# An RWKV-6 layer with a ternary-weight feed-forward: each weight load cut into two or four DMAs

## The reference

```
h = layernorm(x)
xr, xk, xv, xw = tm_* h + (1 - tm_*) h_prev          # token shift
r = sigmoid(xr Wr^T); k = xk Wk^T; v = xv Wv^T; w = -softplus(-(xw Ww^T)) - 1e-4
per head of 64:  o_t = r_t (s + exp(u + k_t) v_t^T);  s = exp(w_t) s + k_t v_t^T
x = x + (groupnorm(o) * ln_w + ln_b) * r  Wo^T
h = layernorm(x)
x = x + bitlinear(silu(bitlinear(h, w_gate)) * bitlinear(h, w_up), w_down)
```

## Time and profile before

| | us |
|---|---|
| median of 2 runs | 13519.63 |
| lowest, highest run | 13518.7, 13520.57 |
| profiled execution | 13554.92 |
| its span, slowest core (core 2) | 13553.3 |
| spans of the 8 cores | 13446.1 to 13553.3 |

### The profile page before, as it was taken

How to read it: one execution, slowest core, us unless ns; L and a number is a source line. 1 busy time by engine, 2 the same in 40 slices (tenths; PEclk the granted TensorE clock), 3 DMA queues, 4 the chain that set the end, 5 groups by cost and what they waited for, 6 DMA issues and landing times.

```text
span 13553.3 us, 44159 instructions; the slowest of 8 cores (13446.1 to 13553.3 us)
## 1 busy us (share of the span) xinstructions
PE 2850.1 (21%) x14044; PEld 1163.0 (9%) x14220; DVE 4326.3 (32%) x3858; ACT 2275.1 (17%) x2088; POOL 170.7 (1%) x60
## 2 busy tenths in 40 slices
PE   0000000012223231323132313241324031412231
PEld 0000000001101110111011101110111010101010
DVE  0010101013263416241624172407240724163326
ACT  0011011113111211121112112210221022102210
POOL 0000000000000000000000000000000000000000
PEclk9999999995666566657565756575657565756576
DMA  2221212220111011101110111010101010101011
GB/s 51 56 70 50 79 51 87 61 71 10 39 33 59 10 40 33 58 10 45 29 56 10 47 29 56 9 53 24 56 9 55 21 56 16 56 25 44 16 56 31
DMA packets 880152, 563.77 MB, mean 42 GB/s; under 512 B 610096, under 2 KB 807088, under 8 KB 877872
## 3 DMA queue, kind: packets, MB, share of 16 engines
q1 hardware_dynamic: 874160, 550.44, 14.0%
q0 software_dynamic: 5760, 10.49, 0.5%
HBM read 424.21 MB, written 52.43 MB: 35 GB/s over the span
## 4 chain that ended last, share of the span: by engine, by line
DVE 28%; SPq 19%; PE 18%; ACT 14%; DMA 14%; issue 4%; DVEq 2%; POOL 1%; ACTq 0%; POOLq 0%; another core or an unknown queue 0%
DVE arn L1394 6%; SPq L363 6%; PE ps L1292 5%; DMA arnb<-wqtu 4%; PE ps L1299 4%; DVE arn L1392 3%; SPq L225 3%; ACT L1312 2%; SPq L473 2%; SPq L1247 2%; PE ps L1447 2%; SPq L1414 2%; SPq L806 2%; DMA arnb<-arnb 2%; PE ps L568 2%
## 5 line engine op out<-in xcount | busy, mean ns | idle before, releaser
L1292 PE MATMUL ps<-arnb 128*128 128x512 bf16 x2000 | 680.6, 497 | 2557.5 <-DMA arnb<-wqtu 1960.9
L1447 PE MATMUL ps<-arnb 128*128 128x512 bf16 x2008 | 534.5, 430 | 2624.9 <-DMA arnb<-arnb 1712.1
L1322 DVE SCALAR_TENSOR_TENSOR arn<-ps,arn 128x512 f32<-128x512 f32 x256 | 192.2, 751 | 2673.8 <-ACT arn L1312 2673.8
L1394 DVE TENSOR_TENSOR arn<-arn 128x2048 f32<-128x2048 f32 x384 | 880.1, 2292 | 29.6 <-issue 1.3
L1312 ACT ACT_TABLE_LOAD x256 | 328.4, 1283 | 2489.5 <-PE ps L1299 2489.5
L568 PE MATMUL ps<-arnb 128*128 128x512 bf16 x1505 | 408.1, 422 | 1299.8 <-DMA arnb<-wtr 1207.4
L349 DVE SCALAR_TENSOR_TENSOR arnb<-arn,thr,arnb 128x1024 bf16<-128x1024 f32 (+1 forms) x72 | 118.1, 1640 | 1666.4 <-ACT arnb L337 1666.4
L1299 PE MATMUL ps<-arnb 128*128 128x512 bf16 x2016 | 544.6, 416 | 3.0 <-issue 1.5
L333 ACT ACT_TABLE_LOAD x72 | 92.4, 1283 | 2582.4 <-DVEq L310 1084.2
L280 PE MATMUL ps<-cpool_s,arn 128*1 128x1 f32 x6 | 0.6, 163 | 2373.8 <-DVE arn L274 2373.8
L1392 DVE TENSOR_SCALAR arn<-arn 128x2048 f32<-128x2048 f32 x384 | 471.2, 1227 | 30.0 <-issue 0.9
(11 more groups left out here) (163 smaller groups left out, 6037.1 us busy)
## 6 DMA issues: line engine op xcount, KB each, us to landing
arnb<-wqtg SPq DMA_DIRECT2D x64, 1024.0 KB, 5.5
arnb<-wqtu SPq DMA_DIRECT2D x64, 1024.0 KB, 8.0
arnb<-wqtd SPq DMA_DIRECT2D x64, 1024.0 KB, 10.3
arnb<-arnb SPq DMA_TRANSPOSE x2880, 2.3
arn<-wg SPq DMA_DIRECT2D x64, 512.0 KB, 3.9
arn<-wu SPq DMA_DIRECT2D x64, 512.0 KB, 3.7
arn<-wd SPq DMA_DIRECT2D x16, 2048.0 KB, 10.2
arn<-x SPq DMA_DIRECT2D x8, 2048.0 KB, 7.8
```

The lines of the kernel that those rows point to most:

```text
L1292: t.matmul(ps[:, bg * 512:(bg + 1) * 512], bass.AP(AR16.tensor, 2 * O_B6 + kc * 512 + g * 128, [[PIT16, 128], [1, 128]]), bass.AP(AR16.ten ...
L1394: v.tensor_add(YF, YF, BF)
L1447: m = t.matmul(ps[:, b * 512:(b + 1) * 512], bass.AP(AR16.tensor, 2 * GT[g] + kc * 128, [[PIT16, 128], [1, 128]]), bass.AP(AR16.tensor, 2 ...
```

## The change

A helper `wload` issues one load as up to `pieces` DMAs of `nblk // pieces` blocks of 128 rows, all on the same semaphore. The stage loads are cut into four column quarters. Addresses, bytes, order and waits are the same.

```diff
+        def wload(sy, dst_off, dst_bs, src_h, src_off, pstride, nblk, inner,
+                  sem, pieces=4):
+            per = max(1, nblk // pieces)
+            for s in range(0, nblk, per):
+                n = min(per, nblk - s)
+                P.inc(sy.dma_start(
+                    out=bass.AP(AR16.tensor, dst_off + s * dst_bs,
+                                [[PIT16, 128], [dst_bs, n], [1, inner]]),
+                    in_=bass.AP(src_h.tensor, src_off + s * 128 * pstride,
+                                [[pstride, 128], [128 * pstride, n],
+                                 [1, inner]])), sem, 16)
```

Both stage loads (L257, L322):

```diff
-                    P.inc(sy.dma_start(out=bass.AP(stg.tensor, stg.offset,
-                                                   [[PIT, 128], [1, ccols]]),
-                                       in_=src_h[ch * 128:(ch + 1) * 128, :]), qld, 16)
+                    qc_ = ccols // 4
+                    for q in range(4):
+                        P.inc(sy.dma_start(
+                            out=bass.AP(stg.tensor, stg.offset + q * qc_,
+                                        [[PIT, 128], [1, qc_]]),
+                            in_=src_h[ch * 128:(ch + 1) * 128,
+                                      q * qc_:(q + 1) * qc_]), qld, 16)
```

The loads of the tiles, each in place of one `dma_start` (wtk, wtw: of two):

```diff
+                    wload(sy, 2 * O_WWIN, 1024, wtr_h, 0, D, 8, 1024, "qwr")
+                    wload(sy, 2 * O_B1, 1024, wtk_h, 0, D, 4, 1024, "qwk",
+                          pieces=2)
+                    wload(sy, 2 * O_B8, 1024, wtk_h, 512 * D, D, 4, 1024, "qwk",
+                          pieces=2)
+                    wload(sy, 2 * O_WWIN, 1024, wtv_h, 0, D, 8, 1024, "qwv")
+                    wload(sy, 2 * O_B1, 1024, wtw_h, 0, D, 4, 1024, "qww",
+                          pieces=2)
+                    wload(sy, 2 * O_B8, 1024, wtw_h, 512 * D, D, 4, 1024, "qww",
+                          pieces=2)
+                    wload(sy, 2 * O_B1, 1024, wto_h, 0, D, 8, 1024, "qwo")
+                        wload(sy, 2 * wgo, 512, wqtg_h, fc * 512, FF, 8, 512,
+                              qwin)
+                        wload(sy, 2 * wuo, 512, wqtu_h, fc * 512, FF, 8, 512,
+                              qwin)
+                        wload(sy, 2 * WDQ[qr], 512, wqtd_h, qr * 1024 * D,
+                              D, 8, 512, "qwd", pieces=2)
+                                wload(sy, 2 * WDQ[qr], 512, wqtd_h,
+                                      qr * 1024 * D + 512, D, 8, 512, "qwd",
+                                      pieces=2)
```

More of the change, by code:

```diff
@@ L976, in _ @@
                     P.wait(sy, "sy", "pe")
-                    src = bass.AP(wto_h.tensor, 0, [[D, 128], [128 * D, 8], [1, 1024]])
-                    P.inc(sy.dma_start(out=bfd(O_B1, [[1024, 8], [1, 1024]]), in_=src),
-                          "qwo", 16)
+                    wload(sy, 2 * O_B1, 1024, wto_h, 0, D, 8, 1024, "qwo")
                 wo_q1 = P.cnt["qwo"]
@@ L1332, in _ @@
                     for qr in range(NG):
-                        src = bass.AP(wqtd_h.tensor, qr * 1024 * D,
-                                      [[D, 128], [128 * D, 8], [1, 512]])
-                        P.inc(sy.dma_start(
-                            out=bass.AP(AR16.tensor, 2 * WDQ[qr],
-                                        [[PIT16, 128], [512, 8], [1, 512]]),
-                            in_=src), "qwd", 16)
+                        wload(sy, 2 * WDQ[qr], 512, wqtd_h, qr * 1024 * D,
+                              D, 8, 512, "qwd", pieces=2)
                 wdw_h0 = P.cnt["qwd"]
@@ L1428, in _ @@
                             for qr in range(NG):
-                                src = bass.AP(wqtd_h.tensor,
-                                              qr * 1024 * D + 512,
-                                              [[D, 128], [128 * D, 8], [1, 512]])
-                                P.inc(sy.dma_start(
-                                    out=bass.AP(AR16.tensor, 2 * WDQ[qr],
-                                                [[PIT16, 128], [512, 8], [1, 512]]),
-                                    in_=src), "qwd", 16)
+                                wload(sy, 2 * WDQ[qr], 512, wqtd_h,
+                                      qr * 1024 * D + 512, D, 8, 512, "qwd",
+                                      pieces=2)
                         wdw_q1 = P.cnt["qwd"]
```

16 lines of the change are left out of this document (removed).

## The result

| | before | after |
|---|---|---|
| median of the runs, us | 13519.21 (8 runs) | 13573.02 (9 runs) |
| lowest to highest | 13508.8 to 13522.7 | 13550.3 to 13603.7 |
| spans of the 8 cores | 13446.1 to 13553.3 | 13462.0 to 13589.1 |

The ratio is 1.0041, with a 95% interval of 1.0029 to 1.0053: slower by 0.4%. That lies within the 2% that were forecast and within the range, 51 us above the predicted 13522. It is a small sum of two larger parts of opposite sign: the stages lost more than was forecast, and the tiles gained more, mostly for a reason that the prediction didn't have. The profiled execution of before (13554.9 us) is longer than any of its 8 timed runs, so the two profiles compare stretches better than totals.

The account below looks back on a forecast made before the run. No engine bounds the kernel: it runs as a relay, where only transfers somebody stands still for count. Terms -19, -5, +19, +10 and -3 sum to +2 us on the median 13519.6, forecast 13522 us, range 13410 to 13670.

Parts of the forecast that it names:

- Rival 1: Exposed bursts and stage loads: every extra issue adds 0.42 us in full, 872 issues, +366 us, 13886 us; chance 0.04.
- rival 2: Gate/up bursts: each piece pays its own start in turn, 26 us per burst, 14670 us; chance 0.01.
- the forecast case (+26): Weight-quantising stage loads: first-pass wg/wu +19 us, second-pass +10 us, wd -3 us.
- rival 4: Stage loads: pieces land at the upper bounds, about +150 us, 13670 us; chance 0.09.
- signs of being wrong: Gate/up burst near 11, beyond 20 or under 7.5 us; first-pass last piece over 3 us; PE waiting at L643 or L1118.
- Issue counts and hidden loads: All cut loads: 872 extra exposed issues; 112 hidden ones cost nothing; packets grow by 55,296 stage rows plus 984 issues' completions.
- wg and wu: Stage loads, 64 per pass: +0.3 us each in the first pass (+19 us), +0.15 in the second (+10 us).
- wd: Its 16 stage loads of 2 MB: -0.2 us each, -3 us, bounds -0.4 and +0.5 us each.
- Gate/up: 64 bursts of the gate/up loop: data stay the bound, -0.3 us each, -19 us, bounds -0.6 and +0.4 each.
- what can change is the slow first microsecond: Gate/up burst start: first microsecond with data moves 141 against 365 GB/s, a 0.6 us shortfall a smaller first piece may shorten.
- wqtd, second half: Four exposed loads per tile, data-bound: -0.3 us per burst, within -5 us for 16 bursts shared with wtr.
- wtr: One exposed 2 MB burst per tile: -0.3 us each, within -5 us for 16 bursts shared with second-half wqtd.

Follow-up runs that it names:

- the sixteen pieces: Changed kernel with whole stage loads and the gate/up loads cut in 8 and 8 pieces of 128 KB: 13692.1 us, ratio 1.0115 against the kernel before.

## Why the prediction was right, and where its steps were not

The verdict, no change of 2% in either direction, held, and its main reason did too: bytes and waits stay, the start of a burst is paid once, and each exposed burst can lose or gain only some tenths of a microsecond. Rival 1 (0.42 us per exposed issue, 13886) and rival 2 (a start for each piece, 14670) are out. A part of rival 1 does exist, as the sixteen pieces show, but not at eight. The stages came out between the forecast case (+26) and rival 4 (+150), at +72.

That the time was only 51 us off is partly luck. A gain of 71 us that had no term stood against losses that were sized too low; without it the time would have been about 13573 + 71 = 13644 us (an estimate from the stretches), still in the range. All three signs by which the prediction wanted to be known as right failed: PE's first matmul came 9.2 us after the first issue and not 8.0 to 8.5, the rate behind the slow microsecond was 283 to 299 GB/s in the mean and not 365, and a first-pass load took 3.9 to 4.0 us to DVE and not 3.3 to 3.8. None of its signs of being wrong came in the medians either.

- *Issue counts and hidden loads.* Right. Packets grew by 951200 - 880152 = 71048; 55,296 are rows and 984 x 16 = 15744 are under 512 B and go with the 984 more issues. Nothing waits for wtv, wto or the first half of wqtd.
- *wg and wu.* The term was mis-sized: +29 forecast, +66 measured (+71 in the kernel with only this change). In the first pass two numbers failed. I took 0.33 us for each issue, from a row in which every issue finds an empty queue; behind another they take 0.43. And I took a start of 1.9 us for a 128 KB piece from the whole load, which put its landing at 2.3 us; it landed after 2.5 to 2.6. The constants of the earlier trace rows, 2.8 and 3.5 us, were the better rows, and I used them for the bound only. In the second pass the issues were not the error, they came sooner than I had them; the landing of the last piece was, 2.8 to 3.2 us and not 2.3.
- *wd.* Small, with the sign wrong in sum: +6 in place of -3. The first pass got 0.1 us shorter (8.3 us to DVE), of the sign forecast. In the second the last piece lands 12.6 us after the first issue, and the whole load landed after 12.0. The first issue is held for 4.0 us behind the write in both kernels, and the last of the four goes out at 5.3 us.
- *Gate/up.* The stretch moved as forecast (-32, forecast -19) for a reason that wasn't in the prediction: that is luck. The step "what can change is the slow first microsecond" was right about the start and missed that the middle of the burst would slow down: the wait is 0.6 us longer and not 0.3 shorter, +39 us where the term said -19. I had allowed +0.4 for "completions that disturb the stream", too little. The -71 us of the clock had no term at all. The rows for it were there: the granted clock of 0.50 within a wait stood in the earlier trace rows, and 40-us passes beside 37-us ones stood in the timeline, of which I had read a single pass.
- *wqtd, second half.* No gain (+1 us in 8 tiles in place of -2.5).
- *wtr.* -6 us, more than the -2.5 forecast: its last byte landed 1.5 us sooner and not 0.3, and after that DVE's mix was the later of the two.

The rule of the Trainium skill that speaks against the change ("DMA: Bandwidth & Descriptors", section Bandwidth: batch DMAs to at least 1 MiB) gets the sign right for the gate/up, wg and wu loads, and wrong for wtr, whose 2 MB land sooner in 512 KB pieces. Its size is another matter: cutting 1 MB into 256 KB costs a burst 0.6 us and cutting 512 KB into 128 KB costs 0.4 to 0.7 us, not a further fixed start of 2.6 us per piece, as long as the pieces are issued back to back.

## What to carry to other kernels

Cutting a load into pieces that everybody waits for together gives little: here it moved the time by -0.1% to +1.2%, and of the loads in the chain only wtr landed clearly sooner. A load in the chain is made cheap by issuing it a step ahead, which made the kernel 4.2% and 8.3% faster. When a loop lets PE stand still in each pass, look at the lengths of many passes and not of one. If they differ for the same work, look at the granted clock in long and short ones; a small change of the idle time can then move the time by more than its own length, as 25 us of delay did here. An experiment that adds pure delay tells such an effect from what a change does by itself.

## What the runs showed of the hardware that I had not expected

- A delay of 0.43 us in each of 56 passes made the kernel 0.64% faster, and twice that delay made no difference; the share of short passes went from 0.40 to 0.82 and back to 0.58.
- After a short pass and 12.0 to 12.6 us of idle time of PE the next pass was short in 608 of 616 cases, over ten kernels with and without cut loads; after 13.0 to 14.5 us in 1 of 108.
- A 2 MB load (wtr) landed 10.1 us after its issue as one DMA and 8.6 us after it as four; two loads of 1 MB issued together took 8.4 us as two DMAs and 9.0 as eight.
- 128 writes of 4 bytes each to HBM, 512 bytes in all, landed after 8.9 us and held up the loads behind them.
- Four DMAs of 32 partitions each, together 2 MB, took 12.6 us from first issue to DVE, four of 128 partitions 8.1 to 8.3 us, one of 128 partitions 8.3 to 8.5 us (medians).
- An SP issue behind another took 0.43 us for 128 rows per DMA, 0.47 for 256 KB of 1 KB rows, 0.58 for 1 MB of them, and 4.0 us for a load of wd behind the 1 MB write in 256-byte runs.
